# Dispatched rows laid out as half of the tiles, slot, half of the width, tile and group

## The reference, cut to what matters

```python
grouped = x.reshape(B, g, t, d)                       # 128 groups of 32 tokens
logits = jnp.einsum('bgtd,des->bgtes', grouped, controller)
perm = (logits + tie == max over t).astype(x.dtype)   # one token for each group and slot
dispatched = jnp.einsum('bgtd,bgtes->bgesd', grouped, perm)
inner = jax.nn.relu(jnp.einsum('bgesd,desf->bgesf', dispatched, f1) + bias)
intermediate = jnp.einsum('bgesf,esfd->bgesd', inner, f2)
out = jnp.einsum('bgesd,bgtes->bgtd', intermediate, perm)
```

## Time and profile before

| | us |
|---|---|
| median of three runs | 1418.1 |
| profiled execution, whole time | 1418.37 |
| profiled execution, span | 1416.5 |
| TensorE busy in the span | 1334.9 (94%) |
| VectorE busy | 1096.4 (77%) |
| ScalarE busy | 713.1 (50%) |
| GpSimd busy | 724.0 (51%) |
| dispatch stage, from 1260 to 1308.7 | 48.7 |
| expert loop, from 1308.7 to 1353.7 | 45.0 |
| transposes and combination, from 1353.7 to 1408.3 | 54.6 |

### The profile page before, as it was taken

The page is one execution under the profiler, slowest core; times in us unless marked ns, Lnnn a source line. Parts: engine busy times, 40 slices in busy tenths (PEclk is TensorE's granted clock), DMA queues, the critical chain, the costliest instruction groups (busy, mean ns, idle before and its releaser), DMA issues.

```text
span 1416.5 us, 25256 instructions
## 1 busy us (share of the span) xinstructions
PE 1334.9 (94%) x9885; PEld 1003.6 (71%) x9885; DVE 1096.4 (77%) x1627; ACT 713.1 (50%) x1345; POOL 724.0 (51%) x1009
## 2 busy tenths in 40 slices
PE   9765699999999999999999999999999989998888
PEld 4443577777777787878686868686868667767765
DVE  1359998888888888888888888888888874344567
ACT  1353465555555546464646464656555534423455
POOL 0524446555555656464747474747474654340424
PEclk7878899999999999999999999999999999999999
DMA  9451212121212121212222222212222341030412
GB/s 372 163 183 36 80 42 76 52 72 53 72 53 72 53 72 53 72 53 72 63 69 69 58 73 61 72 53 72 57 62 52 82 146 31 1 105 2 152 39 83
DMA packets 57021, 109.85 MB, mean 78 GB/s; under 512 B 9422, under 2 KB 37574, under 8 KB 55750
## 3 DMA queue, kind: packets, MB, share of 16 engines
q1 hardware_dynamic: 39814, 61.64, 14.6%
q0 software_dynamic: 14848, 41.96, 10.4%
q10 hardware_dynamic: 2240, 4.63, 0.9%
HBM read 98.24 MB, written 9.95 MB: 76 GB/s over the span
## 4 chain that ended last, share of the span: by engine, by line
PE 79%; DVE 13%; issue 2%; another core or an unknown queue 2%; POOL 1%; DMA 1%; ACT 1%; SPq 0%; POOLq 0%; DVEq 0%
PE side_bank L379 48%; PE score_bank L379 28%; DVE cand_val L1108 3%; DVE cand_idx L1109 3%; PE score_bank L732 2%; DVE x_sum L1132 1%; DVE dispatchedT L1287 1%; DMA sc_in<-shared_compress 1%; PE side_bank L732 1%; POOL exp L1357 1%; DVE dispatchedT L1264 1%; POOL v_rows L1328 1%; PE side_bank L530 0%; PE score_bank L588 0%
## 5 line engine op out<-in xcount | busy, mean ns | idle before, releaser
L875 ACT COPY score_row<-score_bank 128x512 f32<-128x512 f32 x512 | 299.6, 590 | 170.4 <-PE score_bank L379 101.3
L1328 POOL DMA_INDIRECT v_rows<-in_V,top_idx x256 | 248.1, 969 | 188.6 <-DVE top_idx L1122 106.3
L1108 DVE MAX8 cand_val<-score_row 128x8 f32<-128x2048 f32 x128 | 291.8, 2280 | 57.8 <-ACT score_row L875 55.4
L1357 POOL TENSOR_SCALAR exp<-exp,exp_bound 128x256 f32<-128x256 f32 x512 | 243.7, 492 | 113.0 <-ACT exp L887 111.8
L1109 DVE FIND_INDEX8 cand_idx<-cand_val,score_row 128x8 uint32<-128x2048 f32 x128 | 292.5, 2285 | 0.0
L379 PE MATMUL score_bank<-keysT_hi,qT_hi 128*128 128x512 f32 x512 | 219.0, 428 | 31.1 <-ACT score_row L875 28.2
L379 PE MATMUL score_bank<-keysT_lo,qT_hi 128*128 128x512 f32 x512 | 205.2, 401 | 0.0
L379 PE MATMUL score_bank<-keysT_hi,qT_lo 128*128 128x512 f32 x512 | 204.8, 400 | 0.0
L887 ACT ACTIVATE exp<-side_bank 128x512 f32<-128x512 f32 x256 | 139.0, 595 | 98.5 <-PE side_bank L379 94.2
L379 PEld LDWEIGHTS score_bank<-keysT_hi,qT_hi 128*128 128x128 f32 x512 | 98.2, 192 | 70.1 <-ACT score_row L875 32.1
L379 PE MATMUL side_bank<-qT_heads,kT 64*128 64x256 f32 x1024 | 146.1, 404 | 1.0 <-ACT exp L887 0.8
(11 more groups left out here) (200 smaller groups left out, 2266.0 us busy)
## 6 DMA issues: line engine op xcount, KB each, us to landing
kT<-den_scratch SPq DMA_DIRECT2D x62, 256.0 KB, 4.3
f_quads<-in_f POOLq DMA_DIRECT2D x32, 256.0 KB, 3.5
comp_then_wqkv_raw<-in_comp SPq DMA_DIRECT2D x6, 1024.0 KB, 17.9
xT_by_step<-in_xTs SPq DMA_DIRECT2D x4, 1024.0 KB, 8.8
keysT_raw<-in_KmT ACTq DMA_DIRECT2D x8, 512.0 KB, 13.4
xT_in<-in_xT SPq DMA_DIRECT2D x16, 256.0 KB
x_sum<-in_x SPq DMA_DIRECT2D x32, 128.0 KB, 2.1
ctxT_in<-in_ctxT SPq DMA_DIRECT2D x16, 256.0 KB
```

The source lines that it names most:

```text
L875: nc.scalar.copy(srow[n // PER % 2][:, i * CB:(i + 1) * CB], scb[n % 3]).then_inc(sem("score_evac"), 1)
L1108: own(nc.vector.max(cv[:, tile, cs], srow[g % 2][:, :]))
L1328: pool.indirect_dma_start(out=vg[:, k, :], out_offset=None, in_=V_rows, in_offset=bass.IndirectOffsetOnAxis(ap=i8[:, tile, k:k + 1], axis=0))\
L1357: last = nc.gpsimd.tensor_scalar(ex[i % NEX][:, k, :], ex[i % NEX][:, k, :], ub[:, k, c:c + 1], E_LO, ALU.min, ALU.max)
```

## The change

The tile keeps its size, and its axes are put in another order: half of the tiles h (0 for the tiles 0 to 15, 1 for the tiles 16 to 31), slot s, half of the width k, tile within the half, group g. Neighbouring slots of one tile, half of the width and group are now 128 numbers (512 bytes) apart, and the 128 columns of one slot are two runs of 64 numbers, 16384 numbers (65536 bytes) apart. Every access to the tile is rewritten for it. No instruction is added or removed, none moves to another engine or another place in its queue, and no wait is changed.

- The copies of the dispatch stage (L979, L1287) read as before and write runs of 4 numbers, 64 numbers apart for k and 128 apart for s; before, they wrote 1024 numbers in one run.
- `expert_in` reads two runs of 64 numbers instead of 32 runs of 4.
- `expert_evac` reads its banks in runs of 64 numbers instead of 4, and writes two runs of 256 numbers instead of 64 runs of 8.
- `inter_transpose` loads weights whose columns are 128 numbers apart instead of 4.

```diff
-        dtt = sb(exl, "dispatchedT", [P, NT, KT, SLOTS, 4])
+        dtt = sb(exl, "dispatchedT", [P, 2, SLOTS, KT, NT // 2, 4])
...
-                        last = mm(pp[q % 2][r, 0:NG], f1q[j % NF][:, k, i * P + F * s:i * P + F * (s + 1)], dtt[:, :, k, 4 * q + s, :], k == 0, k == KT - 1)
+                        last = mm(pp[q % 2][r, 0:NG], f1q[j % NF][:, k, i * P + F * s:i * P + F * (s + 1)], dtt[:, :, 4 * q + s, k, :, :].rearrange("p h n g -> p h (n g)"), k == 0, k == KT - 1)
...
-                        last = nc.tensor.transpose(set2[n % 3][:, c0:c0 + P], dtt[:, n, k, :, g], idn[:, :])
+                        last = nc.tensor.transpose(set2[n % 3][:, c0:c0 + P], dtt[:, 2 * n // NT, :, k, n % (NT // 2), g], idn[:, :])
...
-                src = set2[u % 3].rearrange("p (s i k n g) -> p i n k s g", s=2, i=2, k=KT, g=4)
+                src = set2[u % 3].rearrange("p (s i k h c) -> p i h s k c", s=2, i=2, k=KT, h=2)
...
-                    last = nc.scalar.copy(dtt[:, :, :, s0:s0 + 2, :], src[:, i])
+                    last = nc.scalar.copy(dtt[:, :, s0:s0 + 2, :, :, :].rearrange("p h s k n g -> p h s k (n g)"), src[:, i])
...
-                    last = nc.scalar.copy(dtt[:, n, :, :, :], set4[0][:, :, 0:D].rearrange("p g (k s) -> p k s g", k=KT))
+                    last = nc.scalar.copy(dtt[:, 2 * n // NT, :, :, n % (NT // 2), :].rearrange("p s k g -> p k s g"), set4[0][:, :, 0:D].rearrange("p g (k s) -> p k s g", k=KT))
```

More of the change, by code:

```diff
@@ L1260, in expert_evac @@
                 need(dve, "ffn2_pe", u // 2 + 1)
-                src = set2[u % 3].rearrange("p (s i k n g) -> p i n k s g", s=2, i=2, k=KT, g=4)
+                src = set2[u % 3].rearrange("p (s i k h c) -> p i h s k c", s=2, i=2, k=KT, h=2)
                 for i in range(2):
                     s0 = 4 * u - 2 + 4 * i
-                    last = nc.vector.tensor_copy(dtt[:, :, :, s0:s0 + 2, :], src[:, i])
+                    last = nc.vector.tensor_copy(dtt[:, :, s0:s0 + 2, :, :, :].rearrange("p h s k n g -> p h s k (n g)"), src[:, i])
                 last.then_inc(sem("ffn2_dve"), 1)
@@ L1286, in _ @@
                 if n >= 0:
-                    last = nc.vector.tensor_copy(dtt[:, n, :, :, :], set4[1][:, :, 0:D].rearrange("p g (k s) -> p k s g", k=KT))
+                    last = nc.vector.tensor_copy(dtt[:, 2 * n // NT, :, :, n % (NT // 2), :].rearrange("p s k g -> p k s g"), set4[1][:, :, 0:D].rearrange("p g (k s) -> p k s g", k=KT))
                 if n + 2 < NT:
```

## The result

The changed kernel takes 1426.28 us (median, 1425.1 to 1428.49) against 1418.32 for the kernel before beside it: a ratio of 1.0054, with an interval of 1.0039 to 1.0069. It is slower by 0.54%, 8 us. Its profiled execution took 1425.78 us with a span of 1423.9, 7.4 us longer than the span before.

What follows compares the result with a forecast made beforehand. TensorE was taken to bound the transposes, and TensorE alternating with VectorE's copies the expert loop and dispatch. Four terms of 0 on the profiled 1418.37 us, median 0.27 lower, gave 1418.3 us, range 1414.0 to 1428.0.

Steps and rivals of the forecast that it cites:

- forecast of no change: Whole kernel: all four parts cost nothing, 1418.3 us, from 1415.5 to 1421.1, chance 0.52.
- rival with dearer far columns: Transposes: weight loads with columns a large power of two apart wait longer; 1427.3 or 1436.5 us, chance 0.22.
- second penalty: Transposes: a further cost for the 512-byte step, as large as that assumed for the 16-byte step, +9.0 us.
- Part 1: expert_in in the expert loop: two runs of 64 numbers instead of 32 of 4 change nothing; 0 us.
- Part 2: expert_evac copies in the expert loop: longer runs read and written gain nothing; 0 us.
- Part 3: Dispatch copies: writing runs of 4 numbers 512 bytes apart instead of one run costs nothing; 0 us.
- Part 4: Transposes: loading weight columns 512 bytes apart costs the same as 16 bytes apart; 0 us.
- upper bound of 5.1 us: VectorE's 16 dispatch copies: at most 1.25 ns a jump, +0.32 us a copy, +5.1 us in all.
- rival with the opposite sign: Transposes: far columns are cheaper than neighbouring lines, at most down to the contiguous rate, 1409.3 us, chance 0.13.
- bound of the contiguous rate: Transposes: weight loads cannot become better than contiguous, 35 ns less each over 256, -9.0 us.
- 1.9 us for a stretch at half clock: Start of the expert loop: 64 expert_in records at 56 ns instead of about 26; one stretch more or less.
- last rival: Expert loop: short runs did cost (-1.2 and -1.0 us), and one half-clock stretch less (-1.9); 1414.2 us, chance 0.07.

Runs made afterwards that it cites:

- experiment 4: Kernel before with expert_in's moving operand read from another tile in seven patterns: 32 records took 1.08 us for one run, up to 2.14 for runs of 2.
- Experiments 1 to 3: Changed kernel with transposes at 16-byte step: 1.0008; kernel before at 512-byte step: 1.0068; kernel before with swept steps; changed kernel padded to 528-byte step: 0.9999.
- experiment 2: Kernel before with transposes' weight columns at other steps, four sweeps, four tiles a step: eight transposes took 1.02 us (contiguous) to 1.49 us.

## Why the prediction was right, and where it was not

The time lies in the range (1414.0 to 1428.0), but not by what was forecast. The forecast of no change, 1418.3 us at 0.52, did not come. What came is the rival with dearer far columns, which had 0.22, and the range holds 1426.28 only because its upper end was drawn to take in that rival's 9.0 us. No row showed the price of a second penalty, so that the one assumed was large enough is luck. By its steps:

- **Part 1 (0 us): right.** `expert_in` stayed at 1.08 us, with 0.81 for its weight loads, and experiment 4 shows a single run at the same 1.08. The rule from the Trainium skill (TensorE: Matmul & The Clock Gate, LDWEIGHTS) named there as the reason, 26.7 ns for a load of 32 columns, agrees with the spacing of the records at full clock, (1.08 - 0.27) / 31 = 0.026 us. That the loads are what sets this spacing is not shown by any run: at about half clock 64 records took 3.56 us, twice as long for each, which the rule does not have, and 2.14 us for runs of 2 numbers shows that the moving side can bind as well. One reading of this part does not hold: records overlap without four strips side by side too, since the transposes' records of 284 ns start 120 ns apart.
- **Part 2 (0 us): right.** Copies at 686 and 589 ns, a step of the loop as before.
- **Part 3 (0 us): right.** 1225 and 1012 ns with runs of 4 numbers at 512 bytes. The upper bound of 5.1 us from single numbers was empty for these runs.
- **Part 4 (0 us): wrong, and it is the whole loss.** The step that failed is "the next number is no further to fetch in one step than in another". I took the value at the one step length that the trace had, although the text itself noted that no row showed another. Experiments 1 to 3 show in its place that the price of a load does differ from step to step, though not with how far the columns are apart as such: 1.37 us instead of 1.16 for eight transposes at 512 bytes, 1.16 again at 528. The sentence's exception, a finer structure of the memory, would fit with experiment 2, but which structure stays open. The part would have been better forecast with the second penalty as an equal candidate.
- **The size of the rival.** Its price of a second penalty "as large as the first", 9.0 us, came out as 0.21 us a tile, 6.5 us in the stage. Its reason was that numbers at a large power of two meet in one place. The dear steps are near to that (the four multiples of 256 bytes that were measured, 192 numbers included, and not powers of two as such); that anything meets in one place is not shown, and the still dearer steps of 80, 208 and 336 bytes do not follow from it. The rival with the opposite sign was not empty either: far columns can be cheaper than near ones, 1.09 us at 32 numbers against 1.16 at 4, only 512 bytes is the wrong distance.
- **The bound of the contiguous rate.** 0.11 us a transpose from a stream of four was taken over eight behind a combination, and gave -9.0 us. Measured it is 1.02 us for eight, 0.14 less than at 16 bytes, so -4.5. The starts in the traces show what was mixed. Contiguous transposes follow one another after 109 ns, but the second of a tile starts 166 ns after the first; at 16 bytes these are 120 and 222 ns, at 512 bytes 147 and 248. The prediction compared 0.11, without the first, to 0.145, with it. Like for like the step of 16 bytes costs 17 ns a transpose and not 35, and the second penalty, 0.21 us for eight, is half as large again as the first.
- **The note on cachelines** in the Trainium skill (SBUF — State Buffer, Door 1: The DMA port swizzle) would have steps of 4 and 128 numbers pay alike and steps of 1 and 2 both nothing. That 4 numbers cost more than 1 agrees (1.16 against 1.02). But 4 and 128 take 1.16 against 1.37, and 1 and 2 take 1.02 against 1.15, so in both of these the measurement decides against it for weight loads of float32 numbers.
- **The clock** gave little: the loop grew by 0.24 us, and the first three tiles of the transposes by 0.4. The 1.9 us for a stretch at half clock were somewhat high: 56 ns a record includes the end of the last one and 26 does not; from start to start it is 50 against 26 ns, 1.5 us.
- **Two slips** change nothing: a third of 1.08 us is 0.36 and not 0.3, and the last rival's time is 1414.2, where the range says 1414.0.

## What to carry to other kernels

A layout has a reader on each side, and it is worth asking first which one is on the chain: here the change served a reader with 0.34 us of cover a step and charged one with none. For transposes of stepped float32 columns the step itself is a parameter to choose: keep it off multiples of 256 bytes, if need be by 16 unused bytes a row, and try an even number of 16-byte pieces, as far as the moving operand allows: the contiguous layout, best for the transposes, cost 2.6% in all. Where a trace has only one value of a quantity that the change alters by a factor of 32, "the same" is not the safe guess, and one sweep within a single kernel settles it.

## What the runs showed of the hardware

- The price of a transpose's weight load goes up and down with the step: for eight transposes, 1.02 us contiguous, 1.09 to 1.11 at 32, 64 and 128 bytes, 1.16 at 16 bytes, 1.36 to 1.38 at 256, 512, 768 and 1024 bytes, and 1.49 at 80, 208 and 336 bytes, all at full granted clock.
- The moving side of four matmuls in column strips is as fast with 16-byte runs 4096 bytes apart as with one run (1.08 us for 32 records). It took 1.20 us or more with such runs 512 bytes apart in another tile, about 2 us for single numbers every 16 or 256 bytes, and about 4 us for single numbers every 512 bytes.
- ScalarE and VectorE write runs of 4 numbers 512 bytes apart as fast as one long run (1012 and 1225 ns for 1024 numbers).
